# Swin block on one core: the projections of v, q and k in 64x64 tiles, v into two PSUM banks

## The reference: what is computed

```python
y = roll(_layernorm(x, g1, b1), (-2, -2))          # then cut into windows of 128 tokens
qkv = xw @ qkv_w + qkv_b                            # (128 windows, 128, 96) -> q, k, v of 4 heads
attn = softmax(q * SCALE @ k.T + bias + mask)
o = (attn @ v) @ proj_w + proj_b                    # windows put back, rolled back
x = x + o
out = x + gelu(_layernorm(x, g2, b2) @ fc1_w + fc1_b) @ fc2_w + fc2_b
```

## Time and profile before

| | |
|---|---|
| runs | 223.63, 223.86, 228.16 us; median 223.86 |
| profiled execution | 224.5 us, of which the span shown 222.7 |
| TensorE busy, weight loads | 202.6 us (91%), 123.5 us |
| VectorE, ScalarE, GpSimd busy | 164.7 (74%), 149.6 (67%), 128.2 us (58%) |
| L851, project_v | 64 passes, median 275 ns, from 25.8 to 171.1 us |
| L845, project_qk | 32 passes, median 626 to 641 ns, from 13.1 to 139.7 us |
| L724, values | 8, 597 ns each |
| L524, row maximum, and L735, exponential | 64 each, mean 1223 and 1023 ns |

### The profile page before, as it was taken

One profiled execution on the slowest core, in us unless ns is written; L12 is line 12 of the kernel. 1 busy time (PEld: TensorE's weight loads), 2 busy tenths in 40 slices (PEclk: granted clock), 3 DMA queues, 4 the chain that ended last, 5 costly groups with the idle time before them and its releaser, 6 DMA issues.

```text
span 222.7 us, 10176 instructions
## 1 busy us (share of the span) xinstructions
PE 202.6 (91%) x4376; PEld 123.5 (55%) x4376; DVE 164.7 (74%) x253; ACT 149.6 (67%) x217; POOL 128.2 (58%) x116
## 2 busy tenths in 40 slices
PE   0889775999999999999999999999999999979884
PEld 0854532576576667656765666566557666453221
DVE  3896863676797788878797877787766867857874
ACT  7465366566867678768867776767546654677883
POOL 7775589353339874895689398623642092240840
PEclk9999999799999999999999999999999999999999
DMA  6816427565425542553355134414540000000333
GB/s 202 252 57 171 138 98 203 157 191 176 145 61 169 181 135 68 158 169 106 100 166 149 37 122 122 153 52 132 179 130 4 6 6 7 1 3 0 125 113 141
DMA packets 24292, 25.54 MB, mean 115 GB/s; under 512 B 3556, under 2 KB 21732, under 8 KB 24164
## 3 DMA queue, kind: packets, MB, share of 16 engines
q1 hardware_dynamic: 23496, 24.16, 34.6%
q10 hardware_dynamic: 752, 0.74, 1.2%
HBM read 16.24 MB, written 8.39 MB: 111 GB/s over the span
## 4 chain that ended last, share of the span: by engine, by line
POOL 39%; issue 38%; PE 11%; ACT 4%; DVE 4%; DMA 2%; POOLq 1%; DVEq 0%; ACTq 0%
POOL rstd L376 17%; POOL X L406 5%; POOL parts L394 4%; POOL yn L386 3%; POOL xc L368 3%; POOL X L411 3%; PE ps L966 3%; DMA X<-x_tok 2%; ACT q_rows L740 2%; POOL mean L356 1%; ACT k_rows L740 1%; POOL var L362 1%; PE pq L966 1%; PE pav L996 1%; PE ps L1018 1%
## 5 line engine op out<-in xcount | busy, mean ns | idle before, releaser
L524 DVE TENSOR_REDUCE negm<-ps 128x8 f32<-128x1024 f32 x64 | 78.1, 1223 | 26.3 <-PE ps L900 25.8
L735 ACT ACTIVATE prob<-ps 128x1024 f32<-128x1024 f32 x64 | 65.5, 1023 | 24.2 <-PE ps L929 21.7
L376 POOL TENSOR_TENSOR rstd<-var,neghalf 128x16 f32<-128x16 f32 x16 | 47.4, 2963 | 16.0 <-DVE var L489 15.1
L914 PE MATMUL ps<-rel_j,id_b 96*32 96x512 bf16 x512 | 40.0, 384 | 3.6 <-ACT prob L735 2.4
L949 PE MATMUL pav<-prob,va 128*32 128x128 f32 x1024 | 41.6, 281 | 0.0
L949 PEld LDWEIGHTS pav<-prob,va 128*32 128x32 f32 x1024 | 24.3, 110 | 12.6 <-issue 6.0
L929 PE MATMUL ps<-q_rows,k_rows 64*64 64x128 bf16 x1024 | 27.0, 223 | 1.3 <-DMA q_rows<-m_mid 1.3
L929 PEld LDWEIGHTS ps<-q_rows,k_rows 64*64 64x64 bf16 x1024 | 16.5, 107 | 19.9 <-issue 14.4
L900 PEld LDWEIGHTS ps<-k_rows,q_rows 64*64 64x64 bf16 x1024 | 22.3, 108 | 6.6 <-issue 0.4
L900 PE MATMUL ps<-k_rows,q_rows 64*64 64x128 bf16 x1024 | 25.5, 218 | 0.0
L876 PE MATMUL ps<-rel_i,ident_b 64*64 64x512 bf16 x256 | 25.1, 382 | 0.0
(11 more groups left out here) (134 smaller groups left out, 336.1 us busy)
## 6 DMA issues: line engine op xcount, KB each, us to landing
slots<-parts SPq DMA_DIRECT2D x21, 256.0 KB, 2.5
q_rows<-slots SPq DMA_DIRECT2D x42, 128.0 KB
k_rows<-slots SPq DMA_DIRECT2D x40, 128.0 KB
X<-x_tok SPq DMA_DIRECT2D x8, 256.0 KB, 4.2
y_tok<-res SPq DMA_DIRECT2D x7, 256.0 KB, 2.0
q_rows<-m_hi SPq DMA_DIRECT2D x32, 4.0 KB
q_rows<-m_mid SPq DMA_DIRECT2D x32, 4.0 KB
bias_parts<-rel_parts SPq DMA_DIRECT2D x3, 128.0 KB
```

The lines of the kernel that those rows point to most:

```text
L376: pool.tensor_tensor(rstd[:, i, :], var[:, i, :], neghalf[:], ALU.pow).then_inc(rstd_done[i], 1)
L524: dve.tensor_reduce(dst, first_home(j)[:].rearrange("p (a u n) -> p a u n", u=2, n=TOK), AX.X, ALU.max, negate=True).then_inc(max_done, 1)
L735: act.activation(prob[:, j % NPROB, :], ps2[:], ACT.Exp).then_inc(exp_done, 1)
L914: pe.matmul(ps2[32 * c:32 * (c + 1), 512 * e:512 * (e + 1)], id3_b[0:96, :], rel_j[0:96, c, e].unsqueeze(2).to_broadcast([96, 2, 2, TOK]), ...
```

## The change

project_qk is cut into four calls of 64 weight rows and 64 output rows, over 512 columns as before. project_v is cut into 16 calls: for each g, two halves of 64 tokens (c) and two halves of the weight (u), of which only the diagonal 64x64 blocks are used; half u goes to bank u (Q0 or Q1), 64 columns for each g. So v's windows lie in another order, and values and weighted_values number the slots of va anew. As v now writes Q1, project_v waits until the m_mid that reads it is done, and transpose_max, which writes Q1 too, waits until values has read v.

```diff
             def values(n):
...
-                act.activation(va[:, n % 2, 16:].rearrange("p (n c) -> p n c", c=32)[:, :, 0:HD],
-                               Q0.rearrange("p (n c) -> p n c", c=HD), ACT.Copy).then_inc(va_done, 1)
+                dst = va[:, n % 2, 16:].rearrange("p (u i c) -> p u i c", u=2, c=32)[:, :, :, 0:HD]
+                src = pq[:].rearrange("p (u x) -> p u x", u=2)[:, :, 0:256].rearrange("p u (i c) -> p u i c", c=HD)
+                act.activation(dst, src, ACT.Copy).then_inc(va_done, 1)
...
             def project_qk(n, banks):
                 pe.wait_ge(yT_done, n + 1)
-                for u in range(2):
-                    mm = pe.matmul(banks[u], wqk[64 * u:64 * (u + 1), :], yT[64 * u:64 * (u + 1), n % 2, :],
-                                   start=True, stop=True)
+                for c in range(2):
+                    for u in range(2):
+                        rows, cols = slice(64 * u, 64 * (u + 1)), slice(64 * c, 64 * (c + 1))
+                        mm = pe.matmul(banks[u][cols, :], wqk[rows, cols], yT[rows, n % 2, :], start=True, stop=True)
                 mm.then_inc(qk_done, 1)
 
             def project_v(n):
+                pe.wait_ge(mmid_done, max(PPI * n // 2, 1))
                 for g in range(NG):
-                    mm = pe.matmul(Q0[:, 128 * g:128 * (g + 1)], yT[:, n % 2, 128 * g:128 * (g + 1)], wv[:],
-                                   start=True, stop=True)
+                    for c in range(2):
+                        at = 128 * g + 64 * c
+                        for u in range(2):
+                            rows = slice(64 * u, 64 * (u + 1))
+                            mm = pe.matmul((Q0, Q1)[u][64 * c:64 * (c + 1), 64 * g:64 * (g + 1)],
+                                           yT[rows, n % 2, at:at + 64], wv[rows, rows], start=True, stop=True)
                 mm.then_inc(vp_done, 1)
 
             def transpose_max(k):
                 pe.wait_ge(max_done, 2 * k + 2)
                 if k:
                     pe.wait_ge(mmid_done, k)
+                    pe.wait_ge(va_done, min((2 * k + 1) // PPI + 1, B))
...
-                        at = 16 * (1 - wi) + ((g * GW + wx) * HEADS + h) * 32
+                        at = 16 * (1 - wi) + (((wx // 2 * NG + g) * 2 + wx % 2) * HEADS + h) * 32
```

## The result

The changed kernel took 228.31 us (median of four executions, 227.82 to 228.56) against 223.94 before: a ratio of 1.020, 95% interval 1.017 to 1.022. I had forecast 221.2 and a range of 218.7 to 224.3, so the range misses it by 4 us and the direction is wrong. The profiled execution took 228.6 us, its span 226.8, 4.1 more than before. In the experiments executions of one kernel spread by 0.4 to 12 us; medians there, and ratios with their 95% intervals, are taken over those within 1.5% of the fastest of their kernel.

A forecast was written before the change was run, and what follows sets the result against it. TensorE's gapless groups were taken as the bound. Four v gains (2.0), three q, k gains (0.3) and the start (0.4) made 2.7 us off the profiled 224.5, so 221.8, or 221.2 as median; range 218.7 to 224.3.

The forecast's parts named there:

- The prices of the groups: TensorE's projections: v takes 0.60 us against 1.09, 0.5 saved each; q and k save 0.1 each.
- The rival of tiles that take turns: TensorE: column tiles on the same 64 rows cannot stream together, q and k take 1.87 us; 228.0 us, chance 0.06.
- The new wait: project_v waits for the subtraction m_mid on VectorE; this eats 0.1 us and no more.
- The cover of ScalarE: ScalarE's values and oT end at 88.4, before the next exponential's scores at 88.5; if cover fails, 0.1 us a period.
- the wait for va_done: transpose_max waits until values has read v; over 1 us lies between.
- The start: v of image 0 ends some 0.7 us earlier, moving SyncE's first scatter; gain between 0 and 0.7, taken as 0.4.
- What passes to the end: Over the periods, four v groups gain 2.0 us and three q, k groups 0.3; groups before SyncE-gated scores gain nothing.
- The clock: A second half-speed stretch of TensorE in the steady part would cost about 1.5 us; 222.7 us, chance 0.03.
- What was to be seen: Signs in the trace, among them a period of 20.4 us instead of 21.0 between 65 and 128.
- the fast bound of the forecast: Whole kernel at the forecast's favourable bounds, start up to 0.7 us and each v up to 0.6: 220.3 us.

The follow-up runs named there:

- half of v: Kernel before with project_v computing only two of its four groups: 220.87 us against 225.22, ratio 0.981.
- the other order: SyncE's HIGH gathers moved to s = 6, MID gathers to s = 0 of the next image, behind the row maxima: kernel after 221.56 us, kernel before 224.47.
- The third chip: Kernel after, unchanged, run again beside the kernel before on another chip: 229.73 us, ratio 1.018.
- the two that padded: Kernel before with seven long-set waits ahead of each second bias: 224.24 us; with seven more ahead of each first bias: 237.93 us.
- the shifts: Long-set waits ahead of TensorE's first matmul: kernel after with 128, ratio 0.983, with 64, 1.023; kernel before with 128, 0.989.

## Why the prediction was wrong, step by step

**The prices of the groups: right.** v 0.62 us (0.60 forecast), q and k 1.02 (1.01); fp32 passes in four 64x64 tiles do run together, a round every 0.058 us, and their loads hide. The rival of tiles that take turns had named 228.0, as it came, but by a cause that the timeline excludes.

**The new wait: slightly wrong.** It costs v 0.09 more than I took, so 0.4 gained and not 0.5.

**The cover of ScalarE and the wait for va_done: right.** The exponential after v starts behind an idle 0.17, as before.

**The start: right in sign, and worth nothing.** The first scatter left at 28.30, 0.5 earlier, and v at 43.06 in place of 44.54. A wait of 1.07 us for the maxima took it back: the scores start at 59.92, before at 59.91. The term of 0.4 measured 0.

**What passes to the end: here it failed.** I wrote of the sends of maxima "1.2 to spare, more than the 0.6 I take out", and "DMA issues are neither added nor moved". The 1.2 us came from the rows of one period, in which no scatter was met by a fetch; the queue's times were taken as fixed. I had seen slow issues (2.69 and 3.23 us for three) and called them things that might "fall elsewhere", without asking what made them slow. Each of them met a fetch of TensorE, at 132.1 and 136.8, as 180 of the 197 slow gather issues of all traces did, and the term for what 224 more passes, with as many loads, do to the fetch traffic was priced at nothing. In the traces the waits grew from 1.3 to 7.1 us, and this took the place of a gain that was there: 4.3 us for half of v, which saves its instructions too, and 2.9 for the change in the other order.

**The clock: named, at the wrong odds.** I gave 0.03 to a second half-speed stretch because TensorE does not idle in the steady part. It does once the maxima are late: 1.58 us before 82.47, and 1.5 us of the loss followed. The third chip shows the loss without it.

**What was to be seen.** The period between 65 and 128 was to shrink from 21.0 to 20.4; from 65.60 to 89.71 it is 24.1. Only between these two rows, where no maxima were waited for, is it 20.5:

```profile
111.51 0.69 PE L858 MATMUL pq<-wv_s,yT 64*64 64x64 f32 x32
...
132.01 0.69 PE L858 MATMUL pq<-wv_s,yT 64*64 64x64 f32 x32
```

That alone told that the gate, not the group, had changed.

**A slip.** By its own terms (0.7 + 4 x 0.6 + 0.3, taken off 223.9) the fast bound of the forecast is 220.5, not 220.3. Nothing hangs on it.

**Open.** How one packet of 0.9 us delays a landing by 1.1 us on average and up to 2.2 was not tried; nor why executions of one kernel spread over up to 12 us on some chips, which fetches that drift against scatters would explain but no run shows. No kernel added v's instructions at no cost of time: of the two that padded, one added half and one slowed TensorE, so that more instructions at another phase turn the gain round is argued from the other side (half of v), the shifts and the count above, and not shown by itself. The half-v kernel also lacks the new wait; that the wait is harmless rests on the other order.

## What to carry to other kernels

A cut into smaller tiles has a price outside its engine: the instructions have to be fetched, through DMA engines that carry the kernel's own transfers. Before calling a queue's slack sufficient, look at its slowest period, ask of every slow issue what else was on the DMA engines, and keep short transfers that gate the bottleneck ahead of long issues and of waits for landings. Here that order was worth 5.5 and 8.8 us on two chips, and only with it was the finer tiling worth 3.

## What the runs showed of the hardware

TensorE's program came in 16 KB packets on a queue of its own, each 0.88 to 1.65 us long in the kernel after, one for every 253 to 257 records of TensorE on average, some 5 us apart. A scatter of 256 KB that met one landed in 3.5 us on average, the others in 2.4. A DMA issue of SyncE that met one took 0.8 to 2 us in place of 0.6 in half of the cases. Waits put on TensorE's program were folded two to an instruction, and each such instruction stands in the trace with 0.05 us, one every 0.11 us: four ahead of the second bias hid under the matmuls (0.46 us from weighted values to bias, as before), eight for each pair did not (237.93 us against 224.94). Rounds of four 64x64 tiles with 64 fp32 columns follow each other in 0.058 us.
